# Hybrid block on one core: both heads of an attention tile in neighbouring PSUM banks, drained by one instruction, and the VectorE work around it in another order

## The reference

```python
def _L0_attn_b_ref(x_q, w_q, w_k, w_v, w_o):
    q = jnp.einsum('ntc,hdc->nhtd', x_q, w_q)
    k = jnp.einsum('ntc,hdc->nhtd', x_q, w_k)
    v = jnp.einsum('ntc,hdc->nhtd', x_q, w_v)
    a = jnp.einsum('nhtd,nhsd->nhts', q, k) / math.sqrt(q.shape[3])
    a = jnp.where(causal_forbidden[None, None], -jnp.inf, a)
    a = jax.nn.softmax(a, axis=3)
    y = jnp.einsum('nhts,nhsd->nthd', a, v).reshape(a.shape[0], t, -1)
    return y @ w_o

x = x + _L0_attn_a_ref(_layernorm(x, axis=-1))
x = x + _L0_ffn_ref(_layernorm(x, axis=-1), gate_w, w1, w2)
x = x + _L0_attn_b_ref(_layernorm(x, axis=-1), w_q, w_k, w_v, w_o)
x = x + _L0_ffn_ref(_layernorm(x, axis=-1), gate_w, w1, w2)
```

## Time and profile before

| | |
|---|---|
| median of 3 runs | 2251.08 us (2250.07 to 2251.12) |
| the profiled execution's own time | 2248.06 us |
| its span, first to last instruction | 2246.3 us |
| TensorE busy | 2132.8 us, 95% of the span |
| VectorE, GpSimd, ScalarE busy | 1403.4, 1383.7, 939.8 us |
| granted TensorE clock, mean | 0.99 |
| attention (units 0 to 30) | about 640 to 1790 us of the span |

### The profile page before, as it was taken

The page is one execution under the profiler, slowest core; times in us unless marked ns, Lnnn a source line. Parts: engine busy times, 40 slices in busy tenths (PEclk is TensorE's granted clock), DMA queues, the critical chain, the costliest instruction groups (busy, mean ns, idle before and its releaser), DMA issues.

```text
span 2246.3 us, 37109 instructions
## 1 busy us (share of the span) xinstructions
PE 2132.8 (95%) x13666; PEld 1604.2 (71%) x13666; DVE 1403.4 (62%) x3215; ACT 939.8 (42%) x1780; POOL 1383.7 (62%) x1242
## 2 busy tenths in 40 slices
PE   7998999999999999999999999899999899999998
PEld 5446888889766656766657666567666578889997
DVE  7375687776656566465764566765665736975654
ACT  6203543454344444244443344442444425434443
POOL 4313575777356676456674566664576756777774
PEclk9999999999999999999999999999999999999999
DMA  4524454555310001011001101100100135445552
GB/s 132 183 94 142 120 134 103 141 146 147 93 25 29 20 20 57 10 46 50 29 29 38 39 29 39 48 29 11 49 28 29 39 113 132 126 101 160 122 144 45
DMA packets 133796, 172.43 MB, mean 77 GB/s; under 512 B 16872, under 2 KB 109040, under 8 KB 133616
## 3 DMA queue, kind: packets, MB, share of 16 engines
q1 hardware_dynamic: 109040, 136.47, 18.7%
q0 software_dynamic: 24576, 33.57, 8.7%
HBM read 130.03 MB, written 39.85 MB: 76 GB/s over the span
## 4 chain that ended last, share of the span: by engine, by line
PE 72%; DVE 10%; issue 4%; POOL 3%; ACT 2%; DMA 1%; SPq 1%; another core or an unknown queue 0%; POOLq 0%; DVEq 0%; ACTq 0%
PE psum L1326 12%; PE psum L1477 11%; PE psum L1455 11%; PE psum L1347 11%; PE psum L1397 7%; PE psum L1502 4%; PE psum L1422 4%; PE psum L1411 4%; PE psum L1458 3%; PE psum L1487 3%; DVE f_hhi L2196 1%; DVE f_hlo L2198 1%; DVE t_neg L2257 1%; PE psum L1294 1%; DVE f_junk L2038 1%
## 5 line engine op out<-in xcount | busy, mean ns | idle before, releaser
L1761 ACT ACTIVATE t_p<-psum 128x512 f32<-128x512 f32 (+3 forms) x768 | 327.4, 492 | 328.5 <-PE psum L1458 316.6
L2458 POOL TENSOR_TENSOR t_acc<-t_acc,t_p 128x1024 f32<-128x1024 f32 (+3 forms) x256 | 421.4, 1646 | 32.1
L2377 POOL TENSOR_TENSOR f_wlo<-f_wst,f_whi 128x256 fp32r<-128x256 f32 x256 | 221.7, 926 | 153.5 <-ACT f_whi L1691 153.4
L1347 PE MATMUL psum<-f_whi,f_hhi 128*128 128x256 f32 x992 | 286.1, 288 | 6.9 <-DVE f_hlo L2198 6.9
L1347 PE MATMUL psum<-f_whi,f_hlo 128*128 128x256 f32 x992 | 280.3, 283 | 0.0
L1347 PE MATMUL psum<-f_wlo,f_hhi 128*128 128x256 f32 x992 | 280.2, 282 | 0.0
L2196 DVE CAST f_hhi<-f_h 128x512 fp32r<-128x512 f32 x256 | 142.7, 557 | 210.7 <-ACT f_h L1711 157.1
L2458 POOL TENSOR_TENSOR t_acc<-t_p 128x768 f32<-128x768 f32 x64 | 135.2, 2112 | 221.0 <-ACT t_p L1761 221.0
L1711 ACT ACTIVATE f_h<-psum 128x512 f32<-128x512 f32 x256 | 153.2, 599 | 277.2 <-PE psum L1326 243.1
L1477 PE MATMUL psum<-t_p,t_v 128*64 128x512 f32 (+3 forms) x1536 | 268.2, 491 | 0.2
L1477 PEld LDWEIGHTS psum<-t_p,t_v 128*64 128x64 f32 x1536 | 104.9, 137 | 160.7 <-issue 133.7
(11 more groups left out here) (301 smaller groups left out, 4608.4 us busy)
## 6 DMA issues: line engine op xcount, KB each, us to landing
f_wst<-in_L_ffn_w SPq DMA_DIRECT2D x64, 1024.0 KB
t_wk<-wkT SPq DMA_DIRECT2D x32, 256.0 KB, 2.6
t_wq<-wqT SPq DMA_DIRECT2D x32, 256.0 KB, 2.8
t_wv<-wvT SPq DMA_DIRECT2D x16, 512.0 KB, 3.7
normal<-f_xy SPq DMA_DIRECT2D x5, 1024.0 KB, 10.2
a_x<-in_L_attn_a_x SPq DMA_DIRECT2D x4, 1024.0 KB, 7.7
res<-a_x SPq DMA_DIRECT2D x32, 128.0 KB, 3.5
t_xy<-res SPq DMA_DIRECT2D x4, 1024.0 KB, 6.4
```

Source lines behind the costliest of these rows:

```text
L1347: m = pe.matmul(out, h[:, js], w[:, f, :], start=(f == 0 and a == 0 and j % 2 == 0), stop=(f == FT - 1 and a == 2), skip_group_check=True)
L1761: act.activation(p[:, i, q0:], k.bank[bank][:, q0:], ACT.Exp, scale=1.0 / float(np.sqrt(k.DH))).then_inc(k.drained[bank], 1)
L2377: m = pool.tensor_tensor(t["wlo"][n % 2][:, i, ks], t["wst"][:, i, ks], t["whi"][n % 2][:, i, ks].bitcast(F32), ALU.subtract)
L2458: pool.tensor_tensor(acc[:, :, q0:], (p0 if kt == 1 else acc)[:, :, q0:], p[:, :, q0:], ALU.add).then_inc(k.p_acc, 1)
```

## The change

- The two heads of a score tile, and of a maximum, now get two neighbouring banks at a time (`work_pair`): (0,1), (2,3) or (4,5). Where the ring stands on bank 7, or on the odd bank of a pair, that bank is passed over. The pair is filled and drained as one: one semaphore step for both heads.
- ScalarE takes one exponent over both banks. VectorE takes one full maximum over both in stretch 1; the masked maxima stay one instruction for each head, but release the pair at the end of the second.
- The fourth product of a score tile is a method of its own, `score_shift`. In the first tile of a unit it is issued behind M0, and only it waits for `t_neg`.
- `last_work`: `max_rows(u + 1)` now stands ahead of `qk_low(u + 2, 0)` on VectorE; `normalize(u, 0)` stands here, behind `qk_low(u + 2, 2)`. Its `divide(u, 0)` is issued ahead of `weigh` in stretch 2, where before both stood at the end of stretch 1.
- The layer norms' steps are no longer issued behind stretch 1; the output products go out four at a time and later (`due`, `ready`).
- The first unit's maxima, which are computed inside the first expert layer, start one expert earlier, on banks 6 and 7, one part at a time instead of two. Three steps of routing are merged with their neighbours.

```diff
+    def pair(self, bank):
+        return self.psum[:, bank * BANK:(bank + 2) * BANK].rearrange("p (i q) -> p i q", i=2)
...
         def row_halves(u, g):
             for i, (c, kt) in enumerate(k.stretch_tiles(g)):
                 self.scores(u, c, kt)
+                if i or g:
+                    self.score_shift(u, c, kt)
                 if u + 1 < U:
                     self.row_max(u + 1, *maxima[g][i])
                     self.part_max(u + 1, *maxima[g][i])
+                if not (i or g):
+                    self.score_shift(u, c, kt)
                 yield
...
             if g == 0 and u:
                 self.divide(u - 1, 1)
+            elif g == 2 and u + 1 < U:
+                self.divide(u, 0)
             for c, kt in k.stretch_tiles(g):
                 self.weigh(u, c, kt)
                 self.add_up(u, c, kt)
-            if g == 1:
+            if g == 1 and u + 1 == U:
                 self.divide(u, 0)
                 normalize(u, 0)
...
         def last_work(u):
             if u + 2 < U:
-                yield from project(u + 2, 0)
+                self.qk_product(u + 2, 0)
             self.max_rows(u + 1)
+            if u + 2 < U:
+                self.qk_low(u + 2, 0)
+                yield
+                yield from project(u + 2, 2)
+            normalize(u, 0)
             yield
-            if u + 2 < U:
-                yield from project(u + 2, 2)
-            yield from pieces(3)
+            yield from pieces(KPC)
+            ready()
...
     def take(self, key, bank, n=1):
-        k = self.k
-        if self.uses[bank]:
-            self.wait_ge(k.drained[bank], self.uses[bank])
+        for b in range(bank, bank + n):
+            self.wait_free(b)
         self.uses[bank] += 1
...
+    def work_pair(self):
+        while True:
+            i, ring = self.work % len(self.work_ring), self.work_ring
+            self.work += 1
+            if ring[i] % 2 == 0 and ring[i] + 1 in ring[i + 1:i + 2]:
+                self.work += 1
+                return ring[i]
...
-        for i in range(2):
-            bank = self.wait_filled(("st", u, c, kt, i))
-            act.activation(p[:, i, q0:], k.bank[bank][:, q0:], ACT.Exp,
-                           scale=1.0 / float(np.sqrt(k.DH))).then_inc(k.drained[bank], 1)
+        bank = self.wait_filled(("st", u, c, kt))
+        act.activation(p[:, :, q0:], k.pair(bank)[:, :, q0:], ACT.Exp,
+                       scale=1.0 / float(np.sqrt(k.DH))).then_inc(k.drained[bank], 1)
...
+        if c != n // k.KPC:
+            dve.tensor_reduce(mx1[:, :, n - k.KPC:n - k.KPC + 1], k.pair(bank)[:, :, 0:w], AX.X,
+                              ALU.max).then_inc(k.drained[bank], 1)
+            return
```

More of the change, by code:

```diff
@@ L860, in normalize, with ready @@
                     self.out_load(b, c)
-                extra.append(output(b, c))
+                due.append(output(b, c))
+        def ready():
+            extra.extend(due)
+            due.clear()
         def row_halves(u, g):
@@ L929, in route @@
                 yield
-            for step in (self.thresholds, self.threshold_rows, self.compare, self.rank, self.positions):
-                step(2, early)
-                yield
+            self.thresholds(2, early)
+            yield
+            self.threshold_rows(2, early)
+            self.compare(2, early)
+            yield
+            self.rank(2, early)
+            self.positions(2, early)
+            yield
             while not state["last"]:
@@ L966, in first_unit @@
             yield from project(0, 0, 2, 1, 3)
-            while self.turned < 2 * k.E - 1:
+            for part in sum(maxima, []):
+                self.row_max(0, *part)
+                self.part_max(0, *part)
                 yield
-            self.work_ring = [6, 7, 0, 1]
-            parts = sum(maxima, [])
-            for n in range(0, len(parts), 2):
-                for part in parts[n:n + 2]:
-                    self.row_max(0, *part)
-                    self.part_max(0, *part)
-                yield
+                if self.turned == 2 * k.E - 1:
+                    self.work_ring = [6, 7, 0, 1]
             self.out_weights()
@@ L995, in units @@
                     column_halves(u, g)
-                    pump(state["rows"])
                     if g != 1:
+                        pump(state["rows"])
                         for n, _ in enumerate((last_work if g else first_work)(u)):
@@ L1049, in __init__, with wait_free @@
         self.uses = [0] * 8
+        self.last = {}
         self.work = 0
+    def wait_free(self, bank):
+        if bank in self.last:
+            by, n = self.last[bank]
+            self.wait_ge(self.k.drained[by], n)
     def take(self, key, bank, n=1):
-        k = self.k
-        if self.uses[bank]:
-            self.wait_ge(k.drained[bank], self.uses[bank])
+        for b in range(bank, bank + n):
+            self.wait_free(b)
         self.uses[bank] += 1
-        k.where[key] = bank, self.uses[bank]
+        for b in range(bank, bank + n):
+            self.last[b] = bank, self.uses[bank]
+        self.k.where[key] = bank, self.uses[bank]
         return bank
@@ L1418, in row_max @@
         self.wait_ge(k.a_qk, 2 * k.NC * u + (2 if n < k.KPC else 4))
-        banks = [self.take(("max", u, n, c, i), self.work_bank()) for i in range(2)]
-        for i, bank in enumerate(banks):
+        bank = self.take(("max", u, n, c), self.work_pair(), 2)
+        for i in range(2):
             hd = k.head_rows(i)
-            pe.matmul(k.bank[bank][:, 0:w], heads["qhi"][hd, n * P:(n + 1) * P], heads["khi"][hd, c * BANK:c * BANK + w],
-                      start=True, stop=True).then_inc(k.filled[bank], 1)
+            m = pe.matmul(k.bank[bank + i][:, 0:w], heads["qhi"][hd, n * P:(n + 1) * P],
+                          heads["khi"][hd, c * BANK:c * BANK + w], start=True, stop=True)
+        m.then_inc(k.filled[bank], 1)
     def max_rows(self, u):
@@ L1448, in scores, with score_shift @@
                 self.wait_drained(("qk", u, j))
-            self.wait_drained(("rows", u))
-        banks = [self.take(("st", u, c, kt, i), self.work_bank()) for i in range(2)]
-        neg = t["neg"][:].rearrange("p n j -> p (n j)")
+        bank = self.take(("st", u, c, kt), self.work_pair(), 2)
         for a, (keys, queries) in enumerate((("khi", "qhi"), ("khi", "qlo"), ("klo", "qhi"))):
-            for i, bank in enumerate(banks):
+            for i in range(2):
                 hd = k.head_rows(i)
-                pe.matmul(k.bank[bank][:, q0:], heads[keys][hd, ks], heads[queries][hd, qs], start=(a == 0), stop=False)
-        for i, bank in enumerate(banks):
+                pe.matmul(k.bank[bank + i][:, q0:], heads[keys][hd, ks], heads[queries][hd, qs], start=(a == 0),
+                          stop=False)
+    def score_shift(self, u, c, kt):
+        k, pe = self.k, self.e
+        q0, qs, _ = self.score_slices(c, kt)
+        bank, _ = k.where["st", u, c, kt]
+        neg = k.t["neg"][:].rearrange("p n j -> p (n j)")
+        self.wait_drained(("rows", u))
+        for i in range(2):
             hd = k.head_rows(i)
-            pe.matmul(k.bank[bank][:, q0:], k.ones[hd, :].bitcast(F32R), neg[hd, qs], start=False,
-                      stop=True).then_inc(k.filled[bank], 1)
+            m = pe.matmul(k.bank[bank + i][:, q0:], k.ones[hd, :].bitcast(F32R), neg[hd, qs], start=False, stop=True)
+        m.then_inc(k.filled[bank], 1)
     def weigh(self, u, c, kt):
```

54 lines of the change are left out of this document (26 added, 28 removed).

## The result

The changed kernel took 2335.31 us (median of 4 runs, 2330.72 to 2340.11), the kernel before, run beside it, 2251.10 us (4 runs, 2250.07 to 2251.80). The ratio is 1.0375, with a 95% interval of 1.035 to 1.040: 84 us slower, where 59 were forecast. The profiled execution took 2340.11 us with a span of 2338.4, against 2246.3 before: 92 us to be found. It is the slowest of the four.

The account below looks back on a forecast made before the run. TensorE, busy 95% of the span, was taken as the bound. 14 + 10 + 11 + 12 + 12 = + 59 us on 2251 gave 2310 us; own range 2287 to 2332 (chance 0.56), 2248 to 2336 for 8 in 10.

Parts of the forecast that it names:

- 32 us of waits, 10 of clock and 4 of tails: Unit boundaries: what could be had there, from waits for `t_neg`, low clock and pipeline tails.
- The chain on VectorE: Boundary: `t_klo`, `t_qlo` and three denominator instructions precede M0's maximum, freeing M0's pair for S2 at T0 + 3.8.
- T0: Boundary: the time at which S0 could start, 0.23 us after the last projection matmul starts.
- Case B: 20 of 30 boundaries: M0 gets the denominators' bank; S2 at T0 + 4.2, divide at T0 + 6.55, 1.15 us later.
- case A: A third of units: denominators' bank not in M0's pair; S2 at T0 + 3.9, divide at T0 + 5.85, 0.45 us later.
- + 0.9: Common boundary: the weighted delay of the divide over both cases, in us, the removed wait's gain included.
- 14 + 10 + 11: Boundaries, us lost: 16 common ones, 6 with the routing's search or its like, 8 without a wait before.
- The 10 us stay: Clock: 2.5 us `t_neg` waits go, 3 to 4 us waits for M0's pair come in the same six units.
- more low clock: Rival, chance 0.08: new short waits at boundaries add low clock, 25 us more, about 2335 us.
- + 12 and + 12: Pairs in stretches 1 and 2: 0.4 us longer each, over 31 units, 12 us for each stretch.
- lower end of 0: Pairs in stretch 1: no added time if the release costs nothing.
- upper bounds of + 0.8 and + 0.7: Pairs: most that stretch 1 (waiting for both engines in full) and stretch 2 could lengthen, in us.

Follow-up runs that it names:

- e3: Kernel before with only max_rows ahead of qk_low and the `t_neg` product of a unit's first tile behind M0: 2228.34 us against 2246.34.
- e5: Kernel before with max_rows ahead of qk_low alone, the `t_neg` product left ahead of M0: 2226.99 us against 2250.11.
- e8: Changed kernel with normalize(u, 0) moved to the first step of last_work, divide still in stretch 2: 2287.73 us against 2250.11 for the kernel before.
- e1: Changed kernel with single banks, exponents and maxima for each head again: 2272.47 us against 2246.34 for the kernel before.
- e4: Kernel before with only the pairs of banks, merged exponents and merged maxima: 2303.33 us against 2246.34.
- e9: Kernel before with bank 7 left out of the attention's round, six single banks, nothing merged: 2317.56 us against 2245.41.
- e6: Kernel before with banks given out in neighbouring pairs, nothing merged, each head's bank released by itself: 2319.97 us against 2250.11.
- e10: Kernel before with the rest of the change: later output products in fours, norm steps, merged routing steps, first unit's maxima earlier: 2251.60 us against 2245.41.
- e11: e5 and e10 joined, with single banks and the denominators where they were: 2223.12 us against 2245.41 for the kernel before.
- e2: Changed kernel with the first chunk's divide and normalize back at the end of stretch 1: 2281.86 us against 2246.34 for the kernel before.
- e12: e11 with merged exponents, scores on pairs (0,1) and (2,3), all else single on banks 4, 5, 7: 2295.21 us against 2245.41 for the kernel before.

## Why the prediction was right in its sign and short in its size

**The removed wait.** Right that it goes, wrong in what that gives. The prediction counted 32 us of waits, 10 of clock and 4 of tails as what can be had at the boundaries. e3 and e5 give 18 and 23 us. In e3, 11 us reappear as waits of M0 for `t_qlo`, `t_qhi` and `t_p`, and the clock's loss stayed at 10.2.

**The chain on VectorE.** The mechanism holds step by step: `t_qlo` and the three instructions ahead of M0's maximum, M0 waiting for the first transpose where it has the denominators' bank (1.18 us at unit 4), S2 behind both. M0's maximum was put at T0 + 3.2, since its pair was to be free at 3.8; it starts at 3.09. Case B had S2 at T0 + 4.2 and the divide at 6.55; the run shows 4.39 and 7.14, the last with the slow clock in it. "About 3.9 us" for a common unit's S2 was the value of case A. The median stretch 0, 6.33 us from an S0 that starts at T0 + 0.09, ends at 6.42 against T0 + 5.41: + 1.0, where the prediction had + 0.9. At the six boundaries that had waited longest, S2 came at T0 + 4.9 to 6.6, where 6.5 was put for all. Summed over units 1 to 30, stretch 0 grew by 63 us and the waits ahead of it shrank by 28: + 35 us, the 14 + 10 + 11 of the forecast. That is in part luck, because 13 us of it are clock's loss, which was costed at nothing; the chain and the waits alone came to some 22. A small slip changed nothing: four output products ahead of S0 take 13.9 us of TensorE, not 7.

**The clock, costed at nothing.** This is the first term that was mis-sized. "The 10 us stay" followed from counting waits of 2.5 us and more. The loss grew to 39.2 us, and e8 ties 27 us of that to the denominators' place. Sorted by the waits ahead of each fall of the clock, 15 us lie behind waits of 1.2 us and less, 17 us behind waits of 1.6 to 3.3 us, and 7 us behind rows of both or at the attention's end; before, it was 7 us behind waits of 2.4 us and more and 3 us at the attention's end.

So the rival *more low clock* had the size of the total (25 us and 2335 us, at 0.08 of the chance), but its mechanism, short waits, made about half of it; the long waits cost more than they had as well. Its objection, that the earlier trace rows show low clock only behind waits of 2.4 us and more, rested on waits of 1.03 us, and says nothing of slightly longer ones: behind M0's waits of 1.18 us, each with one of 0.47 us 1.8 us later, the clock fell in 4 of 11 places in the changed kernel, and behind waits of 1.22 us in e1 in 2 of 15. The Trainium skill, "TensorE: Matmul & The Clock Gate", section "A second HAM failure mode: psum-queue depth-cycling", which the prediction set aside, tells of a bf16 kernel in which short idle spells from cycling through banks make the clock go down and up; the window 780 to 790 of the changed kernel agrees in kind, and most places with the same waits do not. e4 and e9 lost 20.5 and 18.7 us, also with more waits for banks than before.

**The pairs.** Forecast + 12 and + 12 in stretches 1 and 2, and some of the boundaries' cost. e1 and e4 give 57 to 58 us: + 0.60, + 0.46 and + 0.54 us in stretches 1, 2 and 0 (e4), 1.6 x 31 = 50 us, with some of the 10 us of clock's loss in it and some outside. Two things were wrong. The cause: not that the merged instruction frees the first bank late, but that seven banks become six; e6 and e9 lose more without merging (3.1 and 3.2% against 2.5). The prediction walked through three pairs, so the missing bank is in its figure, but its lower end of 0 "if the release costs nothing" gives the bank no price, and with each bank released by itself e6 has + 0.87 us in stretch 1. And the size: stretch 1 is 0.61 us longer in the changed kernel, not 0.4; stretch 2 0.65, not 0.4 (the means over units 1 to 30 give 0.64 and 0.47, 33 us in all against 24). Its upper bounds of + 0.8 and + 0.7 held. An exponent of a pair took 1026 ns, as forecast from the trace's slope, not the 1.15 us that the prediction worked out beside it: the Trainium skill, "ScalarE: Activation LUTs", section "Rules for kernel authors", gives its 0.3 us for an ACTIVATE whose bias is a pointer operand, and the prediction left that condition out.

**The rest, costed at nothing.** + 6 us in e10, and nothing beside e5's order in e11.

**The sum.** By the runs: - 18 for `t_neg`, + 57 for the pairs, + 49 for the denominators, and 0 to + 6 for the rest: + 88 to + 94, against the + 84 measured. The parts interact by a few us, and I did not separate these. Place by place, from unit 1's S0 to unit 31's in the two profiled executions (+ 87 us): the boundaries + 35, as forecast; stretches 1 and 2 + 33, not + 24; and between the stretches about + 18, of which 16 are clock's loss behind stretch 0, not 0. So the + 59 was short by the clock (29 us) and by 9 us of the pairs' price, less the 13 us or so by which the boundaries' chain and waits had been put too high. The measured time lies above the forecast's own range (2287 to 2332) and 1 us inside the wide one.

**Open.** Why the clock falls at some boundaries with case B's waits and not at others. Of the 45 us that TensorE was busy for longer, the 16 that the clock's loss does not cover: such a rest, 11 to 23 us, stands in every kernel here that has lost the round of seven (changed, e2, e4, e6, e8, e9, e12), and is under 6 us in the others, but what it is was not looked into. That merging is good by itself (13 us between e4 and e6) is shown for six banks only.

## What to carry to other kernels

Before two tiles are merged, count the banks that go round before and after: an odd bank that a pair can't use has a price, a ring of six can be tried by changing one line, and here it showed the whole price of the pairs and a little more (3.2% against 2.5). When an instruction is put ahead of a critical one on an engine's queue, look for that engine's idle time first; the three instructions cost 47 us in one place and nothing that could be measured in another, 6 us earlier. And do not cost the clock at nothing where many short waits are new.

## What was not expected of the hardware

- **One bank.** The same kernel on six banks instead of seven lost 72 us of 2245 (e9), although the two kinds of waits that grew (to 48.5 us in all, from 5.9) were 0.4 and 0.3 us long on average and 1.1 at most.
- **Low clock behind short waits.** Waits of 1.18 and 0.47 us, 1.8 us apart, stood ahead of matmuls at a pitch of 0.22 instead of 0.12 us (1.2 GHz for 2.4), at a window's clock of 0.69. It happened in 4 of the 11 places with the first of these waits. The clock's loss went from 10.2 to 39.2 us.
- **The sum of waits does not give the clock's loss.** In one profiled execution each, e3 and e5 have the same four kinds of waits, 17.7 and 17.2 us in all, and lose 10.2 and 3.4 us of clock. The executions of e5 alone differ as much: mean granted clocks of 0.989 to 0.992, where 0.003 of the span is 6.7 us.
- **A read over two banks costs no more than its columns.** 1026 ns for an exponent over 1024 columns in two banks, against 596 for 512 (0.84 ns for each further column, and 0.83 within a bank); 1226 ns for a maximum, against 682 (1.06, and 1.09 for the masked maximum within a bank).
